# Reordering the start and one handover of a fused attention and mixture-of-experts block: first chunk of Wk on ACT's queue, means a chunk ahead, ten zero products, tile 1's high rows ahead of the last norm

## What is computed

```python
x = x + tanh(g_xattn) * xattn(layernorm(x), ctx, Wq, Wkv)    # softmax(q k^T / sqrt(512)) v
x = x + tanh(g_ffn) * ffn(layernorm(x), ...)

# ffn: 8 experts, 2 of them for each token
probs = softmax(x @ gate_w + gate_b, axis=1)                 # over the tokens of a batch
vals, idx = top_k(probs, 2)
h = relu(x @ w1[e] + b1[e]); h = relu(h @ w2[e] + b2[e]); y = relu(h @ w3[e] + b3[e])
v[e] = sum over batches and tokens of y * (weight of e for the token)
out[token] = v[idx0] + v[idx1]
```

## Time and profile before

| | |
|---|---|
| median of 3 executions | 923.37 us (923.28 to 923.46) |
| profiled execution, its own time | 923.53 us |
| span of its trace | 921.8 us |
| instructions | 18677 |
| HBM read, written | 112.95 MB, 31.53 MB |

### The profile page before, as it was taken

One profiled execution on the slowest core, in us unless ns is written; L12 is line 12 of the kernel. 1 busy time (PEld: TensorE's weight loads), 2 busy tenths in 40 slices (PEclk: granted clock), 3 DMA queues, 4 the chain that ended last, 5 costly groups with the idle time before them and its releaser, 6 DMA issues.

```text
span 921.8 us, 18677 instructions
## 1 busy us (share of the span) xinstructions
PE 904.5 (98%) x5650; PEld 850.4 (92%) x5650; DVE 715.9 (78%) x1305; ACT 502.3 (54%) x695; POOL 285.0 (31%) x314
## 2 busy tenths in 40 slices
PE   9999999999999999999999999999999999999985
PEld 6989888888888889999999999999999999999981
DVE  6668888888888787867777777777777777777756
ACT  5354544455444477646666666666666666666521
POOL 4234545655455648721111111111111111110003
PEclk9999999999999999999999999999999999999995
DMA  7434443334432555377757888953753753752009
GB/s 240 161 117 141 155 158 116 114 127 162 157 102 70 141 128 141 98 181 215 194 178 192 243 249 240 250 167 109 190 166 110 193 163 110 192 165 57 17 17 364
DMA packets 105412, 144.95 MB, mean 157 GB/s; under 512 B 29729, under 2 KB 70433, under 8 KB 102177
## 3 DMA queue, kind: packets, MB, share of 16 engines
q1 hardware_dynamic: 97952, 127.15, 45.8%
q0 software_dynamic: 7424, 17.38, 7.1%
HBM read 112.95 MB, written 31.53 MB: 157 GB/s over the span
## 4 chain that ended last, share of the span: by engine, by line
PE 92%; DVE 4%; POOL 1%; issue 1%; ACT 1%; DMA 0%; DVEq 0%; SPq 0%; POOLq 0%; ACTq 0%
PE bank L1429 29%; PE bank L1431 28%; PE bank L1430 28%; DVE x_all L1419 2%; POOL slot_pair L672 1%; PE bank L1555 1%; PE bank L1512 1%; PE bank L1557 1%; PE bank L1574 1%; PE bank L1711 0%; DMA wk_raw<-in_wk_t 0%; PE bank L1443 0%; PE bank L1463 0%; PE bank L1464 0%; PE bank L1504 0%
## 5 line engine op out<-in xcount | busy, mean ns | idle before, releaser
L1429 PE MATMUL bank<-h_hi,w_hi 128*128 128x352 f32 x744 | 241.3, 324 | 0.0
L1431 PE MATMUL bank<-h_hi,w_lo 128*128 128x352 f32 x744 | 240.1, 323 | 0.0
L1430 PE MATMUL bank<-h_lo,w_hi 128*128 128x352 f32 x744 | 239.0, 321 | 0.0
L702 POOL DMA_INDIRECT xg<-xn_dram,idx x72 | 85.2, 1183 | 366.6 <-DMA idx<-slot_pair 351.5
L1007 DVE TENSOR_TENSOR w_lo<-w_raw,w_hi 128x2048 fp32r<-128x2048 f32 (+1 forms) x74 | 165.8, 2240 | 23.9 <-ACT w_hi L879 17.9
L896 ACT ACTIVATE h<-bank,bias 128x352 f32<-128x352 f32 x192 | 96.0, 552 | 138.6 <-PE bank L1431 111.2
L879 ACT ACTIVATE w_hi<-w_raw 128x2048 fp32r<-128x2048 f32 x71 | 135.5, 1908 | 36.8 <-PE bank L1431 32.4
L1007 DVE TENSOR_TENSOR h_lo<-h,h_hi 128x704 fp32r<-128x704 f32 x88 | 78.1, 888 | 84.0 <-ACT h_hi L902 84.0
L1429 PEld LDWEIGHTS bank<-h_hi,w_hi 128*128 128x128 f32 x744 | 139.8, 188 | 0.1
L1430 PEld LDWEIGHTS bank<-h_lo,w_hi 128*128 128x128 f32 x744 | 139.7, 188 | 0.0
L1431 PEld LDWEIGHTS bank<-h_hi,w_lo 128*128 128x128 f32 x744 | 139.3, 187 | 0.0
(11 more groups left out here) (221 smaller groups left out, 1744.0 us busy)
## 6 DMA issues: line engine op xcount, KB each, us to landing
w_raw<-in_w SPq DMA_DIRECT2D x24, 1024.0 KB
xq<-rows_dram SPq DMA_DIRECT2D x80, 176.0 KB
w_raw<-in_w SPq DMA_DIRECT2D x48, 256.0 KB
rows_dram<-xg SPq DMA_DIRECT2D x20, 512.0 KB, 3.3
wb<-slot_pair SPq DMA_DIRECT2D x24, 352.0 KB
xt_raw<-in_x_t SPq DMA_DIRECT2D x16, 512.0 KB, 3.8
c_raw<-in_ctx_t SPq DMA_DIRECT2D x16, 512.0 KB, 4.1
x_all<-in_x SPq DMA_DIRECT2D x16, 512.0 KB
```

Of the source, the lines that this page charges most:

```text
L702: pool.indirect_dma_start(xg[0:n, c], None, rows, bass.IndirectOffsetOnAxis(ap=idx[0:n, c, 0:1], axis=0)).then_inc(gathered, 16)
L1429: pe.matmul(out_ap, lh, rh, start=(i == 0), stop=False)
L1430: pe.matmul(out_ap, lh, rl, start=False, stop=False)
L1431: last = pe.matmul(out_ap, ll, rh, start=False, stop=(i == n - 1))
```

## The change

Five edits. The first chunk of Wk is issued by ACT, as its first instruction, and SP waits until the first chunk of Wq has landed before it issues the other chunks and what follows. `WARM` goes from 14 to 10. On DVE the mean of a chunk is made a chunk ahead of its use (chunks 2 and 3), and `thr_e` and `first_row` go behind `xt_low(0)`. On TensorE, of the low products of a chunk all `wq_hi` x `wk_lo` go first and wait for `wk_lo` alone; only in the last chunk they stay in pairs. On ACT `et_high(1)` goes ahead of `norm2(B - 1)`.

```diff
--- before.py
+++ after.py
@@ -59,7 +59,7 @@
 
 
 
-WARM = 14
+WARM = 10
 
 
 BATCHES = (-1, 3, 13, B - 1)
@@ -428,7 +428,10 @@
 
         @block.sync
         def _(sp):
-            for n in range(DC):
+
+            sp.dma_start(wq_raw[:, 0], wq_t[:, 0]).then_inc(s_wq_in[0], 16)
+            sp.wait_ge(s_wq_in[0], 16)
+            for n in range(1, DC):
                 sp.dma_start(wq_raw[:, n], wq_t[:, n]).then_inc(s_wq_in[n], 16)
                 sp.dma_start(wk_raw[:, n], wk_t[:, n]).then_inc(s_wk_in[n], 16)
             sp.dma_start(xt_raw[:], x_t[0]).then_inc(xt_in, 16)
@@ -748,6 +751,8 @@
 
         @block.scalar
         def _(act):
+            act.dma_start(wk_raw[:, 0], wk_t[:, 0]).then_inc(s_wk_in[0], 16)
+
             def exp(m):
 
                 need(act, nbias_ready, 2 * (m + 1))
@@ -934,8 +939,8 @@
             act.wait_ge(b_in[0], 16)
             relu_half(0, 0, 0)
             relu_half(0, 0, 1)
+            et_high(1)
             norm2(B - 1)
-            et_high(1)
             split_w(0, 1)
             gt_high(B - 1)
             split_w(2, 0)
@@ -984,15 +989,6 @@
             dve.memset(gw[:].bitcast(F32), 0.0).then_inc(s_gw_zero, 1)
             dve.memset(v_sum[:], 0.0).then_inc(v_step, 1)
             dve.wait_ge(v_step, 1)
-            dve.wait_ge(s_conv, 5)
-
-            for n, less in enumerate((TILE, 1)):
-                dve.scalar_tensor_tensor(out=thr_e[:, n], in0=thr[:].unsqueeze(1).broadcast_to([P, E, TILES_MAX]),
-                                         scalar=float(less), in1=ebase[:].unsqueeze(2).broadcast_to([P, E, TILES_MAX]),
-                                         op0=ALU.add, op1=ALU.add).then_inc(s_conv, 1)
-            dve.tensor_scalar(first_row[:], jidx[:], float(TILE), None, ALU.mult).then_inc(s_conv, 1)
-            dve.wait_ge(s_conv, 8)
-
             def stats(src_batch, st, mv, done, step_sem_base):
                 wait_alone(dve, "dve")
                 for c in range(RC):
@@ -1260,13 +1256,25 @@
                 dve.wait_ge(s_wq_sum, n + 1)
                 dve.tensor_scalar(wq_mean[:, n, 1:2], wq_mean[:, n, 0:1], -1.0 / D, None, ALU.mult).then_inc(s_wq_mean, 1)
 
+
             for n in range(DC):
-                wq_minus_mean(n)
+                if n < 2:
+                    wq_minus_mean(n)
+                if 0 < n < DC - 1:
+                    wq_minus_mean(n + 1)
                 dve.wait_ge(s_wq_hi, n + 1)
                 dve.scalar_tensor_tensor(out=wq_lo[:, n], in0=wq_raw[:, n], scalar=wq_mean[:, n, 1:2],
                                          in1=wq_hi[:, n].bitcast(F32), op0=ALU.add, op1=ALU.subtract
                                          ).then_inc(s_wq_lo, 1)
             xt_low(0)
+            dve.wait_ge(s_conv, 5)
+
+            for n, less in enumerate((TILE, 1)):
+                dve.scalar_tensor_tensor(out=thr_e[:, n], in0=thr[:].unsqueeze(1).broadcast_to([P, E, TILES_MAX]),
+                                         scalar=float(less), in1=ebase[:].unsqueeze(2).broadcast_to([P, E, TILES_MAX]),
+                                         op0=ALU.add, op1=ALU.add).then_inc(s_conv, 1)
+            dve.tensor_scalar(first_row[:], jidx[:], float(TILE), None, ALU.mult).then_inc(s_conv, 1)
+            dve.wait_ge(s_conv, 8)
             for n in range(DC):
                 dve.wait_ge(a_his, n + 1)
                 low(a_lo[:, n], bA[n][:], a_hi[:, n], a_los)
@@ -1456,14 +1464,20 @@
                 pe.wait_ge(s_wk_hi, c + 1)
                 for n in range(DC):
                     pe.matmul(bA[n][:], wq_hi[:, c, n * P:(n + 1) * P], wk_hi[:, c], start=(c == 0), stop=False)
-                pe.wait_ge(s_wq_lo, c + 1)
-                pe.wait_ge(s_wk_lo, c + 1)
+                if c < DC - 1:
+                    pe.wait_ge(s_wk_lo, c + 1)
+                    for n in range(DC):
+                        pe.matmul(bA[n][:], wq_hi[:, c, n * P:(n + 1) * P], wk_lo[:, c], start=False, stop=False)
+                    pe.wait_ge(s_wq_lo, c + 1)
+                    for n in range(DC):
+                        pe.matmul(bA[n][:], wq_lo[:, c, n * P:(n + 1) * P], wk_hi[:, c], start=False, stop=False)
+                    continue
+                pe.wait_ge(s_wq_lo, DC)
+                pe.wait_ge(s_wk_lo, DC)
                 for n in range(DC):
                     rows = slice(n * P, (n + 1) * P)
                     pe.matmul(bA[n][:], wq_hi[:, c, rows], wk_lo[:, c], start=False, stop=False)
-                    last = pe.matmul(bA[n][:], wq_lo[:, c, rows], wk_hi[:, c], start=False, stop=(c == DC - 1))
-                    if c == DC - 1:
-                        last.then_inc(a_mm, 1)
+                    pe.matmul(bA[n][:], wq_lo[:, c, rows], wk_hi[:, c], start=False, stop=True).then_inc(a_mm, 1)
             pe.wait_ge(s_pool_const, 5)
             pe.wait_ge(s_half, 2)
```

## The result

The changed kernel takes 926.21 us in the median of its 20 executions. One of them took 5015.81, as did one of the first experiment (5015.85); why is not known. The other 19 took 925.10 to 927.56, with a median of 926.12. The kernel before took 923.93 beside it (922.22 to 926.05, 20 executions). The ratio is 1.0025, with a 95% interval of 1.0017 to 1.0033: slower by 2.3 us, where 0.55 less was forecast. The profiled execution took 927.27, some 1.1 above the median; its span is 925.5, against 921.8.

The account below looks back on a forecast made before the run. TensorE, busy 98% of the span, was taken as the bound. Only the start counted, 0.55 us: profiled 923.53 less 0.55 is 922.98, which lies 0.16 above the median, so 922.9 was forecast, range 921.6 to 924.8.

Parts of the forecast that it names:

- DVE's `thr_e` and `first_row`: DVE before `a_lo`: the moved instructions' 0.6 us just fits 1.15 of idle time; zero, or 0.3 if the cover is gone.
- Wk's chunk by ACT's queue: Start: both first chunks in at about 4.4, first real product at 6.1 against 6.83, chunk 0 done 0.95 ahead of 10.15.
- Rival (c): ACT's start: the 1.28 table load precedes the DMA, wk's first chunk lands at 5.4 to 6.4; 923.1 to 924.0; chance 0.10.
- The hold on SP: SP's queue at the start: wk's second chunk lands at 8.1, chunk 1 starts at 9.6 instead of 10.15, gain 0.55.
- rival (a): Loads at the start: slow restart after SP's wait, +0.4 (923.9) to +2.5 (926.0); chance 0.17, 0.05 of it beyond +1.85.
- what I shifted by 0.7: Landings of context (14.6) and wv (17.8): 0.7 later, range 0 to 2.8; `a_hi` covered by 0.2, wv just covered.
- Later chunks ... arrive faster than that: Start, chunks after wk's second: one is needed per 2.75 us and they arrive faster.
- Ten zero products: TensorE's start: end at 5.45, idle until 6.1 at no cost, removing 0.2 by which the last zero product delayed the first real one.
- rival (b): TensorE's start: the clock rises later because of the idle hole, 923.9 or 925.8; chance 0.10, 0.03 of it beyond +1.85.
- The swap: ACT near 343 us, `et_high(1)` ahead of `norm2(B - 1)`: zero, bounds -0.3 to +0.8, transposes of xn2 covered by 0.6.
- The sum: Whole kernel: profiled 923.53 less 0.55 is 922.98, forecast 922.9; within 0.2% of before at chance 0.80.

Follow-up runs that it names:

- e2: The kernel before with only `thr_e` and `first_row` moved behind `xt_low(0)`: 925.79 us, ratio 1.0019 to the kernel before.
- e3: The changed kernel with POOL's first `c_lo` made to wait for `thr_e` and `first_row`: 923.24 us, ratio 0.9991 to the kernel before.
- e1: The first experiment: the changed kernel with `thr_e` and `first_row` back at DVE's start: 923.25 us, ratio 0.9987 to the kernel before.
- f1: The changed kernel with `norm2(B - 1)` ahead of `et_high(1)` again: 927.36 us, ratio 1.0042 to the kernel before.
- f3: The kernel before with `et_high(1)` ahead of `norm2(B - 1)`, wk's first chunk on ACT and SP's wait for wq's first chunk: 923.54 us, ratio 0.9998.
- f4: The kernel before with `et_high(1)` ahead of `norm2(B - 1)`, wk's first chunk on ACT without SP's wait, and `wk_lo` products first: 922.04 us, ratio 0.9982.
- e4: The kernel before with only `et_high(1)` moved ahead of `norm2(B - 1)`: 922.76 us, ratio 0.9982 to the kernel before.
- h1: The changed kernel with `thr_e` and `first_row` at DVE's start and 14 zero products: 925.01 us, ratio 1.0015 to the kernel before.
- f2: The kernel before with `et_high(1)` ahead of `norm2(B - 1)` and ten zero products for fourteen: 923.12 us, ratio 0.9994 to the kernel before.
- g2: The kernel before with `et_high(1)` ahead of `norm2(B - 1)` and wk's first chunk on ACT, without SP's wait: 921.92 us, ratio 0.9966.
- g1: The kernel before with the last `rn` made ahead of the four sends on POOL: 929.31 us, ratio 1.0041 to the kernel before.

## Why the prediction was wrong

**The step that failed** is "DVE's `thr_e` and `first_row` ... With `xt_low` pinned by x's landing and `a_lo` wanted 0.55 earlier, 0.6 just fits. Zero, and 0.3 if the cover is gone." The cover of 1.15 was idle time of DVE, but it lay under POOL's `c_lo`, which runs from 16.41 to 18.89 in the kernel before. In it an instruction with both inputs in SBUF waits for POOL: 0.43 became 2.60 (after) and 2.61 (e2), and was 0.42 with POOL idle (e3). The timeline of before:

```profile
16.41 2.48 POOL L662 TENSOR_TENSOR c_lo<-c_raw,c_hi 128x1024 fp32r<-128x1024 f32 x1 [2.37 <-ACT c_hi L773]
...
17.79 2.48 DVE L1007 TENSOR_TENSOR a_lo<-bank,a_hi 128x512 fp32r<-128x512 f32 x4 [1.15 <-ACT a_hi L866]
```

The step measured 1.8 us alone (e2 against before) and 2.96 within the change (after against e1). In the profiles x times A moves by 1.71 in the one (20.33 for 18.62) and by 2.32 in the other (21.52 for 19.20), which is half of the difference. That the rest is the fall of the clock, 1.50 in the profiled execution and absent from those of e2 and f1, is argued; it fits that the executions of after spread from 925.1 to 927.6. The "0.3 if the cover is gone" was right for the instructions themselves: 0.24 in e3.

A hint stood in the earlier trace rows: the chain has 1.34 for the first `wq_lo`, while the last takes 0.75 in the same trace. The first ran beside POOL's `wk_lo`, the last while POOL was idle (timeline of before):

```profile
6.32 1.28 POOL L717 TENSOR_TENSOR wk_lo<-wk_raw,wk_hi 128x512 fp32r<-128x512 f32 x1 [3.53 <-ACT wk_hi L859]
...
14.38 0.75 DVE L1266 SCALAR_TENSOR_TENSOR wq_lo<-wq_raw,wq_mean,wq_hi 128x512 fp32r<-128x512 f32 x1 [0.79 <-ACT wq_hi L861]
```

In the kernel after the last runs beside `wk_lo` and takes 1.28. I read 1.34 as the instruction's own duration.

**Wk's chunk by ACT's queue.** Right: first product at 6.13 (6.1), pair at 4.4. Rival (c) is out: the table load moved to 1.23 and the DMA was issued at 0.78.

**The hold on SP.** The landing of wk's second chunk was mis-sized, 8.1 for a measured 8.8, beyond the 8.65 from which rival (a) was to decide. The chunk took 4.0, between the 3.2 and the 5.4. Chunk 1 started 0.06 before its old time, and what I shifted by 0.7 shifted by more: context was issued 2.13 later and landed 2.3 later (16.9 for 14.6), so that `c_hi` went from 15.28 to 16.90 and held `a_hi`, as the forecast said it would if it came late. That is the smaller part of `a_hi`'s 0.71: the product it reads ends 0.56 later (17.68 for 17.12), since the last chunk of A starts at 16.10 instead of 15.59. "Later chunks ... arrive faster than that" failed there: wk's last chunk, issued at 6.64, took 7.7 and landed at 14.3, 3.0 behind the one before it, where one per 2.75 was needed. f3 against f4 prices the hold: some 1.5 us. What the means ahead do within the held order no run separates; `wq_lo` of chunk 2 now stands behind the sum of wq's last chunk, which lands only at 13.48.

**Ten zero products, rival (b).** Neither confirmed nor ruled out. In the profiles with 14 that were read for it (before, e4, h1) the real products are 0.23 apart, but for the first few. With 10 they were 0.43 apart until 9.7 to 9.9 in e1, e3 and f1, until 13 in f2, and at 0.23 from the first real product in after. The extra idle time has its price in some executions; in the medians 0.4 (f2 against e4), less than their intervals tell.

**The swap.** "Zero, with -0.3 to +0.8" missed a gain: 1.2 less (e4), and the same way in after against f1 (1.15 less, within the noise). I read one execution, in which `norm2` did not wait for `rn`; but there `h` had come 1.37 late and had hidden the wait (`rn` was ready at 341.94, `norm2` began at 342.11). The sends ahead of `rn` take 0.97 to 1.64 each, `rn` comes as much as 2.6 us after ACT is free, and with `norm2` first that wait is in front of `et_hi`. e4's 12 executions span 1.8 us, the 35 of before 4.4; that the swap removes the upper group of before is argued from this, as the delay of `h` also varies. The three executions of before that I had, within 0.2, showed nothing of that spread.

**The sum.** The swap -1.24 (e4), the rest of the start +0.49 (e1 against e4, side by side), `thr_e` +2.96 (after against e1, beside medians of before of 923.93 and 924.00): 2.2, for 2.3 measured. These steps lead from the kernel before to the one after, so they add up by construction; the sum shows how the time divides and is no check on it. The forecast had 0, -0.55 and 0. Two slips of its sums change nothing: 922.98 less 0.16 is 922.8, not 922.9, and in (b) chunk 0, nine products of 0.43 and three of 0.23 from 6.1, ends at 10.7, not 10.5. Rival (a) named a slower kernel, but for another reason than the one that decided. g2 and f4, with the swap and ACT's issue but without the hold, the ten zeros and the move of `thr_e`, beat both kernels, at 921.9 and 922.0.

## What to carry to other kernels

Idle time of VectorE is not free room if GpSimd works in it: before an instruction with two SBUF inputs is moved into a gap, look up what GpSimd does there, and the other way round for what GpSimd does beside VectorE. Keeping transfers back to bring one forward shifted every later one here, and the stream moved 10 and 104 GB/s in its first two microseconds; issuing wk's first chunk on ACT's queue without the wait brought it forward by 0.8 (`wk_hi` at 4.76 in g2 instead of 5.54), with the wait by 1.0. Where a wait depends on work whose length varies with what runs beside it, put it behind whatever the bounding engine needs next, and don't judge by one execution.

## What the runs showed of the hardware that was not expected

- A 0.25 us instruction of VectorE was stretched to 2.4 us by one of GpSimd that had started 0.1 to 0.2 before it; VectorE's `a_lo`, with an input in PSUM, was untouched.
- The other way round: GpSimd's indirect DMAs, 0.96 to 1.01 us when alone, took up to 3.06 when they started beside a low part that VectorE makes from two SBUF inputs, and ended some 0.85 after it (before, after, g1).
- TensorE's clock fell after holes of similar size in after (2.45) and h1 (2.13), and not in e2 (2.04) or f1 (2.15, and 2.38 at 349 us). In after it fell about 0.8 us after the products had resumed, in h1 by the time they resumed (0.50 from 344.8 on), and TensorE then worked at the 1.2 GHz level for some 3 us. What decides it no run shows. At the start the granted clock prints 1.00 while the distance of the products then shows the lower level (0.43); after a fall inside the trace it prints 0.50. So at a start the distance is to be read.
- One activation of ACT, with its input there and its engine idle, started 0.04, 1.37 and 2.58 us behind TensorE's last product in three profiles (e1, before, h1). Why is open.
